# Token attention of a four-layer model: mask on diagonal pieces, division behind the weighted sum, exponentials head by head

## What is computed

```python
h = layernorm(x)
logits = h @ w_router.T                      # layer 4: top 2 of 8, weights from their gap
x = x + tanh(g_ffn[1]) * sum_e combine_e * down_e(silu(gate_e(h)) * up_e(h))
qh = layernorm(x).reshape(b, s, 16, 8)       # layer 5: per token
kh = vh = ctx.reshape(b, s, 16, 8)
scores = where(tril(ones(16, 16)), einsum('bsqd,bskd->bsqk', qh, kh) / sqrt(8), -1e18)
x = x + tanh(g_xattn[2]) * einsum('bsqk,bskd->bsqd', softmax(scores), vh)
```

## Time and profile before

| | us |
|---|---|
| median of 3 runs (1651.13 to 1655.38) | 1651.29 |
| the profiled execution | 1648.97 |
| its span in the trace | 1647.2 |
| PE busy in the span | 1186.6 |
| DVE busy | 1185.9 |
| POOL busy | 790.9 |
| ACT busy | 699.4 |

### The profile page before, as it was taken

How to read it: one execution, slowest core, us unless ns; L and a number is a source line. 1 busy time by engine, 2 the same in 40 slices (tenths; PEclk the granted TensorE clock), 3 DMA queues, 4 the chain that set the end, 5 groups by cost and what they waited for, 6 DMA issues and landing times. The chain is left out here.

```text
span 1647.2 us, 31338 instructions
## 1 busy us (share of the span) xinstructions
PE 1186.6 (72%) x9741; PEld 789.5 (48%) x9741; DVE 1185.9 (72%) x3134; ACT 699.4 (42%) x1333; POOL 790.9 (48%) x834
## 2 busy tenths in 40 slices
PE   3788885459989869988886342404899886887886
PEld 1455554136656547756654111101566664544554
DVE  5677876686757635368888787885767565998997
ACT  1455554126656434455555111101566553333332
POOL 0223320003343137677777867873234323776876
PEclk9999998569999889989999665556999998999998
DMA  8455553253545023312112000310444420000000
GB/s 195 60 87 69 72 111 118 33 156 56 81 55 69 17 77 99 95 39 58 46 46 64 24 3 13 50 53 0 66 72 71 58 40 1 1 14 1 13 14 13
DMA packets 95266, 90.99 MB, mean 55 GB/s; under 512 B 8928, under 2 KB 85344, under 8 KB 94816
## 3 DMA queue, kind: packets, MB, share of 16 engines
q1 hardware_dynamic: 91040, 80.98, 26.2%
q0 software_dynamic: 4096, 8.40, 1.7%
HBM read 32.72 MB, written 18.87 MB: 31 GB/s over the span
## 5 line engine op out<-in xcount | busy, mean ns | idle before, releaser
L1533 DVE TENSOR_REDUCE neg_max<-bank 128x4 f32<-128x512 f32 x384 | 252.5, 686 | 129.2 <-PE bank L1053 127.1
L824 ACT ACTIVATE probs<-bank 128x512 f32<-128x512 f32 x384 | 212.5, 596 | 167.3 <-PE bank L1080 166.3
L1051 PE MATMUL bank<-mask_b,ident_b 128*128 128x512 bf16 x384 | 153.4, 400 | 67.0 <-DMA k_rows<-area 37.0
L555 POOL TENSOR_SCALAR rstd_a<-meanvar 128x4 f32<-128x4 f32 x48 | 12.0, 250 | 299.6 <-DVE meanvar L1489 221.0
L1053 PE MATMUL bank<-k_rows,q_rows 96*128 96x256 bf16 x768 | 153.9, 283 | 0.0
L817 ACT ACTIVATE q_rows<-bank 32x512 bf16<-32x512 bf16 x192 | 103.0, 582 | 107.3 <-PE bank L1063 103.9
L606 POOL CAST area<-area 128x1024 bf16<-128x1024 f32 x36 | 37.3, 1036 | 219.8 <-DMA k_rows<-area 167.1
L1070 PE MATMUL bank<-ident_b,mask_b 128*128 128x512 bf16 x384 | 134.3, 391 | 3.0 <-ACT probs L824 1.8
L1080 PE MATMUL bank<-q_rows,k_rows 128*128 128x128 bf16 x1536 | 135.4, 222 | 0.0
L1080 PEld LDWEIGHTS bank<-q_rows,k_rows 128*128 128x128 bf16 x1536 | 112.1, 99 | 27.7 <-issue 2.8
L1094 PE MATMUL bank<-probs,v_aug 128*32 128x128 f32 x3072 | 112.2, 287 | 0.8
(11 more groups left out here) (253 smaller groups left out, 3013.4 us busy)
## 6 DMA issues: line engine op xcount, KB each, us to landing
q_rows<-area SPq DMA_DIRECT2D x144, 128.0 KB
k_rows<-area SPq DMA_DIRECT2D x288, 64.0 KB
ctxT<-ctx_t SPq DMA_DIRECT2D x24, 256.0 KB, 6.7
moe_rows<-m2b SPq DMA_DIRECT2D x4, 1536.0 KB, 13.5
q_rows<-moe_rows SPq DMA_DIRECT2D x24, 256.0 KB, 3.2
moe_rows<-work SPq DMA_DIRECT2D x24, 256.0 KB, 2.4
room<-w_exp SPq DMA_DIRECT2D x1, 4352.0 KB, 13.6
mask_i<-mask SPq DMA_DIRECT2D x8, 256.0 KB, 8.5
```

What stands on the lines that cost most here:

```text
L824: act.activation(probs[j].rearrange("p a b -> p (a b)"), T_BANK[j % 2][:], ACT.Exp).then_inc(exp_done, 1)
L1051: pe.matmul(dst[:], ident_b[:], bcast(mask(b, t), 4), start=True, stop=False)
L1533: dve.tensor_reduce(neg_max[:, 4 * j:4 * j + 4], S_BANK[j % 2][:].rearrange("p (h k) -> p h k", h=4), AX.X, ALU.max, negate=True).then_inc ...
```

## The change

For a token tile: `score` adds the mask only to the four 4 x 4 pieces on the diagonal (the rest of the upper triangle is set to the mask's value once), takes the negated maximum, and subtracts nothing; the exponential is sixteen activations, one per head, each on its own h + 1 scores with the maximum as bias; the scale 1/sqrt(8) is taken into the norm's inverse root; the sum and its reciprocal move into `combine`, which multiplies 128 sums by it instead of `probabilities` 256 weights. The weights have two buffers. `score(n)` now waits for the exponential of n - 1.

Around it: the first token tile is one step earlier (16 tiles lie in expert steps); `gather` stands ahead of `weighted`; the routing of chunks 0 and 1 lies in the two last groups of the attention (`put(1)` right behind it), its scatter goes ahead of POOL's `add_bias` of group 6, and the experts' steps 0 to 5 keep the routing of chunks 2 and 3; the rows of chunk 3 use another buffer, and the second half of chunk 1 is scattered behind `route_std(3)`. The diff, without lines that only rename a bank:

```diff
@@ -59,7 +59,8 @@
-FIRST_STEP = 9
+FIRST_STEP = 8
+TAIL = NK - FIRST_STEP
@@ -205,6 +206,12 @@
+        tok_weights = (tok_e, tok_p)
+        def on_diagonal(at):
+            return at.rearrange("p (b s) -> p b s", s=4 * H + 4)[:, :, 0:4 * H].rearrange("p b (i j) -> p b i j", j=H)[:, :, :, 0:4]
@@ -224,7 +231,7 @@
-            return q_room[0][:, at:at + GT].rearrange("p (t d) -> p t d", t=TG)
+            return (probs_room if c == 3 else q_room[0])[:, at:at + GT].rearrange("p (t d) -> p t d", t=TG)
@@ -356,9 +363,9 @@
-        FFN2_STATS = {15: 0, 16: 1, 17: 2, 18: 3, 20: 4, 24: 5, 28: 6}
-        FFN2_NORM = {16: 0, 17: 1, 18: 2, 19: 3, 21: 4, 25: 5, 29: 6}
-        FFN2_ADD = {17: 0, 18: 1, 19: 2, 20: 3, 22: 4, 26: 5, 30: 6}
+        FFN2_STATS = {16: 0, 17: 1, 18: 2, 19: 3, 20: 4, 24: 5, 28: 6}
+        FFN2_NORM = {17: 0, 18: 1, 19: 2, 20: 3, 21: 4, 25: 5, 29: 6}
+        FFN2_ADD = {18: 0, 19: 1, 20: 2, 21: 3, 22: 4, 26: 5, 30: 6}
@@ -568,14 +575,14 @@
             def token_std(g):
-                inv_std_of(t_meanvar[:, :, 1], t_rstd_a, t_rstd, t_stats_ready, t_rstd_ready, g + 1)
-            def scatter(c):
+                inv_std_of(t_meanvar[:, :, 1], t_rstd_a, t_rstd, t_stats_ready, t_rstd_ready, g + 1, float(DH))
+            def scatter(c, tiles=range(TC)):
...
-                for o in range(2 * TC):
+                for o in (2 * t + k for t in tiles for k in range(2)):
@@ -644,12 +651,13 @@
+                        if a == 1 and left == 0:
+                            scatter(0)
...
-                        if a == 1 and left == 0:
+                        if a == 1 and left == 1:
...
-                            scatter(0)
@@ -737,41 +745,42 @@
             def weighted(n):
...
-                pool.wait_ge(tok_probs, n + 1)
+                pool.wait_ge(tok_exp, n + 1)
...
-                        tok_p[:, 4 * i:4 * i + 4, 0:nj].unsqueeze(2).to_broadcast([P, 4, DH, nj]),
+                        tok_weights[n % 2][:, 4 * i:4 * i + 4, 0:nj].unsqueeze(2).to_broadcast([P, 4, DH, nj]),
...
             def feed_forward1_and_tokens():
...
-                scatter(1)
+                scatter(1, range(TG))
...
+                scatter(1, range(TG, TC))
...
+                pool.wait_ge(scattered[3], 16 * 2 * TC)
...
+                    if g + 1 < NG and t < 2:
+                        gather(g + 1, range(2 * t, 2 * t + 2))
...
-                    if g + 1 < NG:
-                        if t < 2:
-                            gather(g + 1, range(2 * t, 2 * t + 2))
-                        if t == 2:
-                            token_std(g + 1)
+                    if g + 1 < NG and t == 2:
+                        token_std(g + 1)
@@ -846,8 +855,8 @@
-                            if a == 1 and left == 0 and t == 1:
-                                gap_weight(0)
+                            if a == 1 and left < 2 and t == 3:
+                                gap_weight(1 if left == 0 else 0)
@@ -856,6 +865,8 @@
+                            if a == 1 and left < 2 and t == 1:
+                                take_routed(2 - 2 * left)
@@ -864,8 +875,8 @@
-                            if a == 1 and left == 1 and t in (1, 2):
-                                take_routed(t - 1)
+                            if a == 1 and left < 2 and t == 1:
+                                take_routed(3 - 2 * left)
@@ -898,7 +909,10 @@
             def token_exp(n):
...
-                act.activation(tok_e, tok_s, ACT.Exp, scale=DH ** -0.5).then_inc(tok_exp, 1)
+                weights = tok_weights[n % 2]
+                for h in range(H):
+                    ins = act.activation(weights[:, h, 0:h + 1], tok_raw[:, h, 0:h + 1], ACT.Exp, bias=tok_m[:, h:h + 1])
+                ins.then_inc(tok_exp, 1)
@@ -930,11 +944,10 @@
-                    routed = k in (0, 2, 4)
...
-                        if routed and m < 2:
-                            take_routed(k + 2 + m)
+                        if k in (1, 3) and m in (1, 3):
+                            take_routed(k + 3 + m // 2)
@@ -1163,6 +1176,15 @@
+                            if a == 1 and left < 2 and t == 1:
+                                if left == 1:
+                                    pe.wait_ge(prep_read, 8 * NG)
+                                    pe.wait_ge(experts_loaded, 32)
+                                turn_routed(0 if left == 1 else 2)
+                            if a == 1 and left < 2 and t == 2:
+                                logits(0 if left == 1 else 1)
+                            if a == 1 and left == 1 and t == 3:
+                                ranks(0)
@@ -1180,15 +1202,8 @@
-                            if a == 1 and left == 1 and t in (1, 2):
-                                if t == 1:
-                                    pe.wait_ge(prep_read, 8 * NG)
-                                turn_routed(t - 1)
-                            if a == 1 and left == 1 and t == 3:
-                                pe.wait_ge(experts_loaded, 32)
-                                logits(0)
-                            if a == 1 and left == 0 and t == 1:
-                                ranks(0)
+                            if a == 1 and left < 2 and t == 1:
+                                turn_routed(1 if left == 1 else 3)
@@ -1334,27 +1349,25 @@
+                ranks(1)
...
-                turn_routed(2)
...
-                        if m == 0 and k in (0, 2, 4):
-                            turn_routed(k + 3)
-                        if m == 0 and k in (1, 3, 5):
+                        if k in (1, 3) and m in (0, 2):
+                            turn_routed(k + 3 + m // 2)
+                        if m == 1 and k in (2, 4):
...
-                        if m == 2 and k in (0, 2, 4):
-                            logits(k // 2 + 1)
...
-                        turn_routed(k + 3)
+                        logits(k // 2 + 2)
@@ -1613,12 +1626,8 @@
-                            if a == 1 and left == 1 and t == 0:
-                                route_stats(0)
-                            if a == 1 and left == 0 and t == 1:
-                                route_stats(1)
-                            if a == 1 and left == 0 and t == 2:
-                                put(0)
+                            if a == 1 and left == 1 and t in (0, 2):
+                                route_stats(t // 2)
@@ -1639,12 +1648,13 @@
-                            if a == 1 and left == 1 and t < 2:
-                                route_norm(t)
-                            if a == 1 and left == 0 and t == 0:
-                                choose(0)
-                            if a == 1 and left == 0 and t >= 2:
-                                route_norm(t)
+                            if a == 1 and left < 2 and t == 0:
+                                route_norm(0 if left == 1 else 2)
+                                route_norm(1 if left == 1 else 3)
+                            if a == 1 and left < 2 and t == 2:
+                                choose(0 if left == 1 else 1)
+                            if a == 1 and left == 1 and t == 3:
+                                put(0)
@@ -1903,7 +1911,9 @@
             def feed_forward1_and_tokens():
-                dve.memset(tok_raw, 0.0).then_inc(dve_steps, ch.one())
+                dve.memset(tok_raw, MASKED).then_inc(dve_steps, ch.one())
+                for weights in tok_weights:
+                    step(dve.memset(weights, 0.0))
@@ -1925,35 +1935,35 @@
+                put(1)
...
-                    if k in (0, 2):
-                        route_stats(k // 2 + 2)
+                    if k < 2:
+                        route_stats(k + 2)
+                    if k in (2, 4):
+                        choose(k // 2 + 1)
...
-                    if k in (1, 3, 5):
-                        put(k // 2 + 1)
-                    if k in (1, 3):
-                        route_norm(k + 3)
...
-                    if k in (1, 3):
-                        route_norm(k + 4)
+                    if k < 2:
+                        route_norm(2 * k + 4)
+                    if k in (2, 4):
+                        put(k // 2 + 1)
...
-                        probabilities(n)
...
-                    if k in (0, 2, 4):
-                        choose(k // 2 + 1)
+                    if k < 2:
+                        route_norm(2 * k + 5)
@@ -2013,31 +2022,24 @@
             def score(n):
...
+                if n:
+                    dve.wait_ge(tok_exp, n)
...
-                dve.tensor_tensor(tok_s, tok_raw, row("heads_causal").rearrange("p (i j) -> p i j", i=H), ALU.add
-                                  ).then_inc(dve_steps, ch.one())
-                dve.wait_ge(dve_steps, ch.count)
-                dve.tensor_reduce(tok_m, tok_s, AX.X, ALU.max).then_inc(dve_steps, ch.one())
-                dve.wait_ge(dve_steps, ch.count)
-                dve.tensor_tensor(tok_s, tok_s, along(tok_m, H), ALU.subtract).then_inc(tok_shifted, 1)
```

(21 more changed lines are left out.)

16 lines of the change are left out of this document (7 added, 9 removed).

## The result

The changed kernel took **1667.96 us** (median of 16 runs, 1652.29 to 1673.88), the one before 1652.38 (16 runs, 1643.10 to 1658.27) on the same chip: a ratio of **1.008**, 95% interval 1.0057 to 1.0104. The forecast of 1643.3 us, faster, was wrong in its sign, and 1668 lies above the range too. The profiled execution took 1668.7 us, its span 1665.8.

What follows compares the result with a forecast made beforehand. Bounds: ACT and PE waiting for each other in token steps, DVE and POOL in the tail, idle engines before the experts. -9.3 - 8.6 + 25.5 + 2.9 - 19.0 + 0.5 = -8.0 us; forecast 1643.3 us, range 1621 to 1662.

Steps and rivals of the forecast that it cites:

- Step 1: Start of the experts: earlier placing and scatters, covered by the attention, bring the first expert product to 590.4, gaining 9.3 us.
- Step 2: Plain expert steps to first token tile: first score at 691.0, 17.9 ahead; POOL's list takes back 5 us.
- Step 3: Token steps: loops of 14.6 us, so score 0 to score 15 takes 216.4 instead of 190.9, 25.5 lost.
- 0.35 for a lower clock in part of them: Token steps: allowance per loop, in us, for PE's lower clock, added within the loop of 14.6.
- rival C: Token steps: PE's longer standstill brings a lower clock in every loop; 12 us later, 1655 us, chance 0.12.
- Step 4: Tail, weighted product of tile 15 to that of tile 31: 197.9 us instead of 216.9, 19 gained.
- 31.4 for the last four: Tail: time in us for the last four token tiles, part of the sum of 197.9.
- Beside POOL's products here: Tail: the exponential lies beside POOL's products, so the gain of 19 us doesn't come from it.
- The end: Behind the last tile's weighted product: the product behind the last sum costs 0.5 us.
- Rival A: Token steps: bias operand not overlapped, each exponential takes 0.29; 22.5 us later, 1666 us, chance 0.15.
- B: Token steps: bias operand hides completely, spacing 0.11; 19 us earlier, 1624 us, chance 0.18.
- D: Start of the experts: it doesn't move, as the added early routing costs its gain; 7 us later, 1650 us, chance 0.05.

Runs made afterwards that it cites:

- e7: The changed kernel with the first token tile one step later, as before the change: 1663.6 us, ratio 1.007.
- e3: The changed kernel plus 16 unused identity products in each token step where PE stands still: 1653.6 us, ratio 1.0016.
- e12: e3 with the gathers behind the weighted product again in the expert steps: 1649.5 us, ratio 0.9998.
- e4: The kernel before with sixteen exponentials, one per head, without bias operand and with its subtraction kept: 1665.9 us, ratio 1.0078.
- e14: e9 with tile 30's exponentials ahead of feed-forward group 6 on ACT, and that group's DVE addition behind tile 31's score: 1623.7 us.
- e9: The changed kernel with one exponential per tile and, in expert steps, gathers behind the weighted product and the next group's norm ahead of the score: 1627.0 us.

## Why the prediction was wrong, point by point

**Step 1, the start: right in its mechanism, less in the net.** From the attention's last instruction on DVE to the first expert product: 15.2 us before (15.0 to 15.4 in four records of kernels with the old start), 5.4 after (5.2 to 5.5 in thirteen records with the new one). That is 9.8; forecast were 9.3. The work moved into the attention, set at 0 with bounds 0 to 3, does cost: from the attention's first maximum on DVE to its last instruction 231.1 to 238.1 in the four, mean 234.6, and 233.9 to 240.8 in the thirteen, mean 237.4. That is about 3, and it isn't sure, as one and the same code differs by 7 us from record to record. In the pair of records above the first product comes 5.3 us earlier, since the attention ends 4.2 later in the record of after; in the means of the four and the thirteen it comes at 602.1 and 593.9, 8.2 earlier.

**Step 2, up to the first token tile: near in size, wrong in its reason.** First product to first score: 109.2 before, 97.8 after, 11.4 gained; forecast 8.6. The prediction had the moved plain step give 9.4 and POOL's list take most of it back. By e7 the move gives nothing (98.2 without it). What is left is the earlier placing and gathering of step 1; that these make the gain is what remains, not what a run of their own shows.

**Step 3, the token steps: here it failed.** Its terms for the window were right: spacing 0.19 (measured 0.193), sixteen 3.05 (3.18), window 5.65 (5.8). The rest of 8.3 was right as well, for PE at its full clock: 8.3 in most loops of e3 and e12, and their mean loop is 14.5 and 14.3 against the 14.6 forecast. The term that was mis-sized is **"0.35 for a lower clock in part of them"**. The lower clock comes in all of them, the rests of after are 9.0 and 10.1 by turns, and the loop is 15.37: 0.35 should have been 0.9 (against e3's mean loop) to 1.1 (against e12's). From score to score, the forecast without this term had 12 for the first and 14.25 for the other fourteen; e12 at the full clock has 11.6 and 14.4, after 12.8 and 15.5. So the rest of the sum held, and 14 x 0.35 = 4.9 us stood where the clock took 13.5 (e3) to 16.7 (e12). The row was there: in the earlier trace rows the long window has a rest of 9.37, in the earlier trace rows the short one 8.31. The prediction read it, made rival C of it with 0.12, and gave it 0.8 a loop from that one row. PE stood still for 2.2 us there; e4, with 2.3 in each loop, has the same rest of 9.2 to 9.3, while after stands still for 3.8. C was the right mechanism, and about 1.1 its price. Its sentence with the Trainium skill (TensorE: Matmul & The Clock Gate, Part 1), that by the page these stalls would fetch the lower level in each step, is what the trace of after shows: a granted clock of 0.84, with matmuls at half speed in each loop.

What then followed on POOL was shorter than forecast: 12.75 from score 15 to weighted 15, not 14.8.

**Step 4, the tail: half of it.** Gained were 216.9 - 208.0 = 8.9, forecast 19.0. Up to tile 25 the intervals hold within 1.2 us each, 143.6 in sum against the 144.0 of the forecast. Tiles 26 and 27 took 25.2 where 22 was put, and the last four 39.2 where "31.4 for the last four" stood; in the kernel before they took 37.8. This term was made from POOL's and DVE's lists alone. It left out that the exponentials of tiles 30 and 31 are on ACT and DVE behind the chain of feed-forward group 6, which the change doesn't shorten; in e14 the two moves bring the last four from e9's 38.2 to 34.2. What held tiles 26 and 27 wasn't tested. The terms as written also add up to 197.4, not 197.9. "Beside POOL's products here" was true of the sixteen exponentials up to tile 29 only.

**The end.** From the weighted product of the last tile to the end: 518.6 before, 523.5 after; forecast +0.5. The 5 us lie behind the start of the last attention, in code that the change doesn't touch: from its first maximum on DVE to the end 495.2 to 498.3 in the four records with the old order and 497.5 to 500.7 in the thirteen with the new. The two groups overlap. What of it is the change's was not found out, and stays open.

The sum against the predicted span of 1639.2: score 0 +1.2, steps +13.0, weighted 15 behind it -2.1, tail +10.1, end +4.4, together the 26.6 that the span was longer. Rival A (0.29, nothing overlapped) fell, B (0.11) holds only where there is no operand, and D fell.

With the clock held the changed kernel stands at 0.9998 and 1.0016 of the one before. So even with step 3 right the forecast of "faster" would have failed, by the tail and the end.

## What to carry to other kernels

A window in which one engine is busy with something else costs its own length and, if the matmul engine stands still in it, the slower matmuls that follow. Read the rest of the loop behind the longest stall in the record of before, and use it for each loop once every loop has that stall. Cheap passes saved on an engine that isn't the bound (22 us of DVE here) don't pay for a window 2.8 us longer on the one that is. And where an estimate adds up two engines' lists for the end of a stage, follow the third engine's and the in-order places of the last two items.

## What the runs showed of the hardware that was not expected

- More work made it faster: 16 idle products a step (3.7 us of PE) took 13.5 us out of 229.4 (e3) and lifted the granted clock from 0.84 to 1.00.
- A standstill of 3.77 us is followed by some 5 or 3 us of matmuls at half the clock (1.57 instead of 0.83 for six products), in every loop; one of 2.3 us (e4) by some 3 us in every loop; one of about 1 us (before, e9) brings it in some of them only.
- The bias operand adds 0.09 us to each short activation even back to back: 0.19 against 0.10.
- DVE's addition of 64 elements took 0.22 alone and 4.54 beside POOL's four weighted products; its norm of four tiles, 1.12 in most other groups, took 3.85 beside them; a product of 128 elements, 0.29 alone, took 6.09 beside eight of POOL's products in a row.
- The same code reached its first expert product between 587.8 and 597.9 us in thirteen records. A cut is to be read as a difference inside one record, not by its place on the time axis.
